# Constant products on PE in three waits of the first attention's opening

## The reference, cut to what matters

```python
x = x + attention0(layernorm(x), ctx)      # with biases; softmax
x = x + experts(layernorm(x))              # the best of 8 experts per token, 128 -> 512 -> 128
x = x + attention1(layernorm(x), ctx)      # position bias, 1 + sum in the denominator
x = x + spikes(layernorm(x))               # 128 -> 512 -> 128, then 5 steps of a threshold
# attention: q = x Wq, k = ctx Wk, v = ctx Wv; scores = q k^T / sqrt(8); softmax; (p v) Wo
```

## Time and profile before

| | |
|---|---|
| time, median of 3 executions | 382.57 us (382.35 to 384.62) |
| the profiled execution's own time | 381.7 us |
| its span | 379.9 us |
| PE busy | 298.8 us, 79% of the span |
| DVE busy | 276.9 us, 73% |
| ACT busy | 234.1 us, 62% |

### The profile page before, as it was taken

How to read it: one execution, slowest core, us unless ns; L and a number is a source line. 1 busy time by engine, 2 the same in 40 slices (tenths; PEclk the granted TensorE clock), 3 DMA queues, 4 the chain that set the end, 5 groups by cost and what they waited for, 6 DMA issues and landing times.

```text
span 379.9 us, 8980 instructions
## 1 busy us (share of the span) xinstructions
PE 298.8 (79%) x3124; PEld 181.8 (48%) x3124; DVE 276.9 (73%) x688; ACT 234.1 (62%) x521; POOL 147.8 (39%) x230
## 2 busy tenths in 40 slices
PE   1378998899878871699998037799889987898994
PEld 0133444444443360499898012344444444347993
DVE  5787899999994558447483238889989998813676
ACT  2127789888988430365554013788988898865652
POOL 3332653456500301754410678345453520174400
PEclk9999999999999885589999655589999998989999
DMA  5226444223422050344531132112211120000111
GB/s 165 71 61 163 140 125 115 79 47 101 112 60 64 0 169 0 66 127 127 148 60 41 46 83 62 43 43 62 63 29 47 54 64 5 10 2 1 29 41 41
DMA packets 34477, 26.30 MB, mean 69 GB/s; under 512 B 5904, under 2 KB 30352, under 8 KB 34432
## 3 DMA queue, kind: packets, MB, share of 16 engines
q1 hardware_dynamic: 31312, 22.43, 21.1%
q0 software_dynamic: 1248, 2.56, 3.2%
q10 hardware_dynamic: 1872, 0.73, 0.7%
HBM read 13.17 MB, written 4.13 MB: 46 GB/s over the span
## 4 chain that ended last, share of the span: by engine, by line
PE 43%; DVE 15%; ACT 13%; DMA 13%; issue 7%; SPq 3%; POOL 3%; ACTq 1%; DVEq 0%; POOLq 0%
PE M L381 11%; ACT Pt L541 8%; PE R L331 7%; DVE nm L677 6%; PE R L1457 4%; PE M L1475 3%; PE R L1271 3%; DMA sorted_y<-ysb 3%; PE R L1290 3%; DMA Pt<-in_mask 2%; PE R L340 2%; DMA Qt<-mT 2%; PE M L443 2%; PE M L455 1%; PE M L390 1%
## 5 line engine op out<-in xcount | busy, mean ns | idle before, releaser
L677 DVE TENSOR_REDUCE nm<-R 128x2 f32<-128x512 f32 x256 | 164.0, 685 | 19.7 <-PE R L331 17.2
L541 ACT ACTIVATE Pt<-R 128x512 f32<-128x512 f32 x256 | 140.2, 595 | 31.7 <-PE R L340 30.4
L331 PE MATMUL R<-Kt,Qt 32*128 32x256 f16 x512 | 56.5, 303 | 21.6 <-DVE nm L677 13.7
L381 PE MATMUL M<-Pt,Vt 128*32 128x256 f32 x1024 | 72.4, 403 | 0.3 <-ACT Pt L541 0.3
L340 PE MATMUL R<-Qt,Kt 32*128 32x256 f16 x512 | 53.5, 288 | 3.5 <-ACT Pt L541 2.3
L331 PEld LDWEIGHTS R<-Kt,Qt 32*128 32x128 f16 x512 | 15.0, 95 | 64.1 <-DVE nm L677 40.5
L381 PEld LDWEIGHTS M<-Pt,Vt 128*32 128x32 f32 x1024 | 27.7, 113 | 25.9 <-ACT Pt L541 8.9
L1318 ACT ACTIVATE hf<-R,b1c 128x128 f32<-128x128 f32 x92 | 26.2, 367 | 19.7 <-PE R L1271 19.7
L1184 POOL DMA_INDIRECT xt<-normed_x,source x23 | 22.3, 970 | 21.4 <-PE M L1281 16.8
L1271 PE MATMUL R<-x_t,w_t 128*128 128x128 f32 x184 | 28.2, 302 | 0.5 <-DVE x_t L1341 0.5
L1271 PEld LDWEIGHTS R<-x_t,w_t 128*128 128x128 f32 x184 | 24.8, 210 | 1.1 <-issue 0.9
(11 more groups left out here) (166 smaller groups left out, 491.0 us busy)
## 6 DMA issues: line engine op xcount, KB each, us to landing
w_ff<-in_w SPq DMA_DIRECT2D x8, 512.0 KB, 3.9
Pt<-in_mask SPq DMA_DIRECT2D x8, 256.0 KB
Qt<-q_hi SPq DMA_DIRECT2D x28, 64.0 KB, 2.0
Kt<-k_hi SPq DMA_DIRECT2D x28, 64.0 KB, 1.9
sorted_y<-ysb SPq DMA_DIRECT2D x23, 64.0 KB, 2.2
Kt<-k_lo SPq DMA_DIRECT2D x16, 64.0 KB, 2.0
Qt<-q_const SPq DMA_DIRECT2D x16, 64.0 KB, 2.6
Qt<-q_lo SPq DMA_DIRECT2D x16, 64.0 KB, 2.0
```

The lines of the kernel that those rows point to most:

```text
L331: mm = pe.matmul(row_bank(b, h)[:, q, :], Qt[b % NBUF][rows_of(h), h // HG, q * P:(q + 1) * P], Kt[b % NBUF][rows_of(h), h // HG, :], star ...
L381: mm = pe.matmul(o_bank(b)[KB * i:KB * i + KB, tile * S:(tile + 1) * S], Vflat[par][:, at:at + KB], Pt[g][:, i, k * S:(k + 1) * S], start= ...
L541: act.activation(Pt[i // 2][:, 2 * j + hh, :], key_bank(b, 2 * i + hh).rearrange("p k n -> p (k n)"), ACT.Exp, scale=1.0 / SC).then_inc(ly ...
L677: v.tensor_reduce(nm[par][:, h // 8, :, h % HG, h // HG % 2], row_bank(b, h), AX.X, ALU.max, negate=True)\
```

## The change

PE gets products that no one reads. `keep_running(pe, n)` multiplies `ones16` with itself: 128 rows, 128 columns of weights, 512 columns moved (the same 128 columns four times over), written into bank 5 of `R`. It is called in three places of the first attention alone:

- 11 products as soon as DVE has filled `ones16` (`inited` at 3), ahead of the wait for the loads;
- 2 products in slot -2 behind the transposes of the tokens, ahead of the wait for `xnT`;
- 6 products in slot -2 behind the product of the queries, ahead of slot -1.

Nothing is removed and nothing is moved. Bank 5 is first used in earnest by the second pass of sequence 0, which starts its sums afresh, on PE itself. The second attention calls nothing of this, since it has `ly["bias"]` false.

```diff
+        def keep_running(pe, n):
+
+            for _ in range(n):
+                pe.matmul(R[:, 2 * RING - 1, :, :].rearrange("p q n -> p (q n)"), ones16[:, :],
+                          ones16[:, :].unsqueeze(1).to_broadcast([P, 4, P]), start=True, stop=True)
+
...
                     for q in range(QT):
                         mm = pe.transpose(M[0][:, q * P:(q + 1) * P], xn[par][:, q, :], eye[:, :])
                     mm.then_inc(ly["xnT_done"], 1)
+                if s == -2 and ly["bias"]:
+                    keep_running(pe, 2)
                 if gate:
                     gate_products(pe, 0, 2)
                 pair(2)
...
                     pe.matmul(M[0][:, 0:S], W["q", ly["index"]][:, :], xnT[:, :], start=True,
                               stop=True).then_inc(ly["q_done"], 1)
+                if s == -2 and ly["bias"]:
+                    keep_running(pe, 6)
                 pair(3)
...
         @block.tensor
         def _(pe):
+            pe.wait_ge(inited, 3)
+            keep_running(pe, 11)
             pe.wait_ge(loaded, 16 * N_LOADS)
             first_keys_on_tensor(pe, ly[0])
```

## The result

The changed kernel takes 379.75 us (median of 20 executions, 377.02 to 384.45), the kernel before 381.72 (median of 20, from 378.24; the three of the table ahead of the prediction are among them). The ratio of the two is 0.994, with a 95% interval of 0.9915 to 0.9966: faster by 0.6%, some 2 us. It compares only those executions that lie within 1.5% of the fastest of their kernel, so it can differ from a difference of the means, which take in all.

A forecast was written before the change was run, and what follows sets the result against it. The prediction took the opening to be bound by one thread through PE's products at the lower clock; 0.52 us for the keys, 0 for cover and occasionally 0.52 for queries gave 0.5, so 382.57 became 382.05, stated 382.0 (range 380.4 to 383.6).

The forecast's parts named there:

- the mechanism: First attention's opening: added products under PE's waits raise its clock, so the keys take 0.70 us instead of 1.22.
- the cover: PE's wait before the keys, 5.24 us or 0.476 per product; 11 products at 0.43 take 4.73 and cost nothing.
- the price of a product: One added product on PE: 0.43 us at the lower clock, 0.22 at the higher.
- how long it holds: Raised clock: over the keys in most executions, the queries in perhaps a third, down by 17 us at the latest.
- The rival of a held clock: Clock holds through the first attention's opening, slots -1 and 0 included: 5.0 us gained, 377.6 us; chance 9%.
- the sum: Held clock's gain: keys and queries 1.04, slot -1 1.9, slot 0 2.0, together 5.0 us.
- 382.57 becomes 382.05: Step from the assumed median of the kernel before to the changed kernel's, then stated as 382.0.
- some 0.5 us for the spread of executions: Allowance in the forecast range for differences between executions, given beside 382.35 to 384.62 before.
- my range: Forecast time of the changed kernel, 380.4 to 383.6 us, taking in forecast, no rise and partly held clock.
- The sum: Forecast gain: 0.52 us for the keys, 0 for cover, now and then 0.52 for queries; 0.5 as the value.
- now and then: Queries of slot -2 also run at the higher clock in perhaps a third of executions, 0.52 us more gain.
- the rise near 41 us stays: Later clock rise keeps its time, so value products run longer at 1.94 instead of 1.07; up to a third given back.

The follow-up runs named there:

- e6: Changed kernel with more unread products through slots -2, -1 and 0 of the first attention; over two sets -2.5 us (-3.5 to -1.4) against the kernel before.
- after_third: The changed kernel unaltered, timed a third time: mean 381.19 us against 382.23 for the kernel before, ratio 1.0004.
- e7: As e6, with the same products in the second attention's opening and 31 ahead of it; ratio 0.9937 to the kernel before, means -1.23 us.
- e2: Changed kernel without the 11 products, the 2 and the 6 kept; ratio 1.0014 to the kernel before, means -0.73 us.
- before_again: The kernel before, unaltered, run for one more time and a second profile: 380.89 us.

## Why the prediction was wrong, point by point

**Right: the mechanism.** The 11 products start at 1.22 and end ahead of the loads; 22 do not, and hold the keys, so the cover was what made them free. The keys take 0.70 in every kernel with the 11. `xnT` came at 9.31 (near 9.5 forecast). The first rise lay between 4.07 and 6.41 (4 to 7.5 forecast). The 2 and the 6 delayed nothing.

**Right, but not from the rows: the price of a product.** The products are 0.43 us and then 0.21 or 0.22 apart, as taken. The rows only placed them between 0.38 and 0.61 at the lower clock and above 0.24 at the higher: 0.43 was a choice within the first, and 0.22 lies under the second, so no row carried it.

**Right: how long it holds.** I had the keys at full clock in most executions and the queries in perhaps a third: three of three and one of three, though three profiles are few. The clock was down by 14.3, 8.7 and, after a second rise, 14.7 us (by 17 forecast). Slot -1 ran at 1.22 per product, as before. The rival of a held clock did not come true by itself; e6 had to build it. Then the opening was 3.5 us shorter, not 5.0: the sum counted all of slot -1's products, and SP's issues and the `ctxT` load behind them hid part.

Two rules of the Trainium skill, page "TensorE: Matmul & The Clock Gate", bear on this. Its section "Why this matters for your kernels" lays a fall within a kernel to a long idle gap. By the traces the falls in the opening are not of that kind: in after_third the clock fell at 8.66 and in the changed kernel's first profile at 14.31, and the longest gaps ahead of these were 1.04 and 2.17 us. The fall at 208.87 in that first profile agrees with the rule: PE stood idle from 206.48 to 216.63. The page's Part 1, "What's actually happening", says that the number of slow products before the rise differs between runs of one kernel. The traces agree: the changed kernel's three profiles have their first rise at 4.07, 4.45 and 5.25 us, behind products that all began at 1.22.

**Wrong: the last steps, from the sum to the time.** The forecast of 382.0 was missed by 2.25 us: 0.85 of it is the start (382.57 taken, where the median of 20 is 381.72), and 1.40 is the gain (0.57 taken, where the medians differ by 1.97).

The start and the spread are the larger miss, in the steps "382.57 becomes 382.05" and "some 0.5 us for the spread of executions". I took both from three times. The mean of 71 is 381.96, so I started 0.6 us too high even against that; and single times spread by 2 us, not by 0.5, so that the median of one set can lie a full microsecond from the mean of many. The first median of the changed kernel, 379.75, lies 0.65 below my range; the medians of its two later sets, 381.30 and 381.22, and the mean of all 44, 380.86, lie inside it.

The gain was mis-sized as well, by less. The sum took 0.5: the keys' 0.52, the queries "now and then", and up to a third given back because "the rise near 41 us stays". From the keys to the first scores the changed kernel gained 1.04, 0.52 and 0.51 against the mean of the two profiles before, 0.7 in the mean, which is the keys always and the queries once in three. Nothing was given back: the opening as a whole ended 0.86 us earlier (50.19 for 51.05, means of three and two), since the second rise did not stay. It lay at 38.20, 38.59 and 39.38, against 40.84 and 39.55 before. Counted from the first scores it came after 24.07, 23.97 and 24.53 us, against 25.51 and 24.48, so about half of its shift (0.67 of 1.47 us in the mean) is that of the work ahead of it. Whether the other half is more than chance, five profiles cannot tell. In time the three sets measured 1.1 (0.4 to 1.8), an interval that holds both the 0.5 and the 0.86.

Where the spread comes from is shown in part. The rest of the kernel behind the opening took between 325.8 and 331.5 us in fourteen profiled executions, while its instructions were the same in all but e7. In the first set of the changed kernel the time goes with the mean granted clock (correlation -0.85): 377.02 us at 0.869, 384.45 at 0.851. The falls and rises that make this mean lie at other places in each execution, as near 111 us in the second profile of the kernel before and not in the first. That they cause the whole spread was not tried.

**Open.** Whether the first set's 2 us held anything beyond a lucky draw cannot be settled: its interval (0.39 to 2.85 between means) includes 1.1. What the 2 and the 6 add to the 11 is also below what the times can tell: -1.35 us without them, -1.1 with them, both to about 1 us. Nor do the times part the 11 alone from the 2 and the 6 alone (-1.35 and -0.73 on one chip: 0.6 apart, to 1.65 either way); that the early rise is what shortens the opening rests on the profiles and on e6. In the profiles of the changed kernel the 2 and the 6 carried the clock over the queries once in three.

## What to carry to other kernels

Idle time of PE under a load that must be waited for anyway is free room to raise its clock, if the filling ends before the load does; but the gain lasts only as long as the products behind it stay dense, and a raised clock over two products is worth those two products, 1 us here. Before forecasting a change of that size, look how far single executions of the kernel spread: three times, 382.35 to 384.62 here, did not show it, and a set of twenty did. When a stage is sped up further, read the chain again at once: in the first opening it went to SP's issues and a load after 3.5 us, in the second to POOL's gathers after 1.

## What the runs showed of the hardware that was not expected

Products of a constant with itself, written where nothing reads, raise the clock as others do: the first rise came 2.85 to 5.19 us after the first of them. With none ahead of the loads, the query product and six of them behind it, without a gap, were enough for a rise (13.64, e2). The view of the granted clock shows 1.00 ahead of its first event, whatever the level: 28.0 to 39.5 us in before_again reads 1.00 while PE's products there take 1.22 us, as they do at 0.50. So the mean granted clock of two kernels cannot be compared: the kernel before shows 0.904 and the changed one 0.867 in their first profiles, although the changed one was faster.
